# A decoder layer on one core: the next input is split a period earlier, and its first projection is done in two blocks around the turning of the second norm's inputs

## The reference

```
i, f, g = x Wi, x Wf, x Wg
a = sigmoid(f);  b = silu(i) * (1 - a);  h[t] = a[t] h[t-1] + b[t]
xg = h * silu(g);  y = xg * rsqrt(mean(xg^2) + 1e-5) * w_norm
x1 = layernorm(x + y Wo)
x2 = layernorm(x1 + wkv(w, u, key=x1, value=ctx))        # a scan over tokens, numerator / denominator
xq = 8-bit rounding of x2 by row;  weights rounded by row too
hid = silu(xq Wgate) * (xq Wup), rounded by row;  out = layernorm(x2 + hid Wdown)
```

## Time and profile before

| | us |
|---|---|
| three runs | 439.98, 434.78, 437.27 (median 437.27) |
| the profiled execution | 435.36 |
| its span, first to last instruction | 433.4 |
| PE busy in the span | 376.4 (87%) |
| DVE busy | 365.8 (84%) |
| ACT busy | 320.0 (74%) |
| POOL busy | 234.0 (54%) |

### The profile page before, as it was taken

One profiled execution on the slowest core, in us unless ns is written; L12 is line 12 of the kernel. 1 busy time (PEld: TensorE's weight loads), 2 busy tenths in 40 slices (PEclk: granted clock), 3 DMA queues, 4 the chain that ended last, 5 costly groups with the idle time before them and its releaser, 6 DMA issues.

```text
span 433.4 us, 7988 instructions
## 1 busy us (share of the span) xinstructions
PE 376.4 (87%) x2810; PEld 292.3 (67%) x2810; DVE 365.8 (84%) x620; ACT 320.0 (74%) x422; POOL 234.0 (54%) x282
## 2 busy tenths in 40 slices
PE   7799889789898899889997999899989997576872
PEld 7797889687865687659764976497648774232331
DVE  3889797575998799989898988898898989899584
ACT  3687777649827898588858995799668975985571
POOL 1775554542644844766475746594459436635451
PEclk9999999989999999999999999999999999889998
DMA  7946550662020010020203020302030202000101
GB/s 253 363 167 238 164 187 2 232 66 75 2 98 1 2 42 33 24 99 0 74 1 122 3 73 2 121 0 73 0 121 0 73 0 73 24 2 0 49 24 52
DMA packets 12843, 31.75 MB, mean 73 GB/s; under 512 B 2038, under 2 KB 5132, under 8 KB 12812
## 3 DMA queue, kind: packets, MB, share of 16 engines
q1 hardware_dynamic: 12812, 31.35, 21.9%
HBM read 27.14 MB, written 4.21 MB: 72 GB/s over the span
## 4 chain that ended last, share of the span: by engine, by line
ACT 22%; DVE 21%; PE 20%; issue 19%; POOL 12%; DMA 3%; SPq 1%; POOLq 0%; ACTq 0%; DVEq 0%
PE proj_ps L478 15%; POOL ring L1266 3%; PE slot_ps L579 2%; POOL x_low L1189 2%; ACT L978 2%; ACT hqT L943 2%; DVE inp L1459 2%; ACT ring L929 2%; ACT L982 2%; DVE stats L1486 2%; DMA ring<-w_gate_up_dram 2%; ACT turn_ps L883 2%; DMA ring<-w_down_dram 2%; POOL gate L1206 1%; DVE x_max L1575 1%
## 5 line engine op out<-in xcount | busy, mean ns | idle before, releaser
L579 PE MATMUL slot_ps<-w1q,xqT 128*128 128x512 bf16 (+1 forms) x384 | 83.1, 367 | 10.3 <-ACT xqT L920 7.6
L1266 POOL TENSOR_TENSOR ring<-ring 128x512 f32<-128x512 f32 (+1 forms) x48 | 60.5, 1262 | 25.7 <-ACT ring L929 25.7
L579 PEld LDWEIGHTS slot_ps<-w1q,xqT 128*128 128x128 bf16 x384 | 36.7, 99 | 48.7 <-issue 8.1
L478 PE MATMUL proj_ps<-x_high,proj_high 128*128 128x256 f32 x384 | 65.0, 291 | 5.0 <-DVE inp L1478 3.1
L478 PE MATMUL proj_ps<-x_low,proj_high 128*128 128x256 f32 x384 | 62.4, 284 | 0.0
L478 PE MATMUL proj_ps<-x_high,proj_low 128*128 128x256 f32 x384 | 62.0, 283 | 0.0
L478 PEld LDWEIGHTS proj_ps<-x_high,proj_high 128*128 128x128 f32 x384 | 53.4, 190 | 8.1 <-issue 7.1
L478 PEld LDWEIGHTS proj_ps<-x_low,proj_high 128*128 128x128 f32 x384 | 53.3, 191 | 0.0
L478 PEld LDWEIGHTS proj_ps<-x_high,proj_low 128*128 128x128 f32 x384 | 53.2, 190 | 0.0
L929 ACT ACTIVATE ring<-ring,zero_bias,x_scale 128x512 f32<-128x512 f32 (+1 forms) x48 | 36.9, 772 | 13.5 <-DVE ring L1598 13.4
L612 PE MATMUL slot_ps<-w2q,hqT 128*128 128x512 bf16 x176 | 42.5, 390 | 4.5 <-ACT hqT L943 3.5
(11 more groups left out here) (135 smaller groups left out, 849.5 us busy)
## 6 DMA issues: line engine op xcount, KB each, us to landing
ring<-w_gate_up_dram SPq DMA_DIRECT2D x11, 512.0 KB, 5.1
forget<-xT_dram SPq DMA_DIRECT2D x8, 512.0 KB, 3.8
x_sb<-x_dram SPq DMA_DIRECT2D x8, 512.0 KB, 4.0
c_sb<-cT_dram SPq DMA_DIRECT2D x8, 512.0 KB, 4.3
out_dram<-z SPq DMA_DIRECT2D x16, 256.0 KB, 2.1
ring<-w_down_dram SPq DMA_DIRECT2D x4, 704.0 KB, 5.4
scale_rows<-scratch_dram SPq DMA_DIRECT2D x2, 704.0 KB, 7.1
x<-wfT_dram SPq DMA_DIRECT2D x2, 512.0 KB, 5.7
```

What stands on the lines that cost most here:

```text
L478: last = nc.tensor.matmul(out, a, b, start=(i == 0), stop=(i == len(terms) - 1))
L579: last = nc.tensor.matmul(slot_ps[:, s, half * 512:half * 512 + width], xqT[:, par, d, t * P:(t + 1) * P], w1q[:, d, half * I + at:half * ...
L1266: nc.gpsimd.tensor_tensor(hid, hid, gate_buf[:, at:at + width], ALU.mult).then_inc(hid_ready, 1)
```

## The change

The split of the input of batch `b + 3` is moved from the head of period `b + 1` to the end of period `b`. On ACT it stands behind the last silu of the period; on POOL behind the last `hidden` and ahead of `rstd_1`. On PE, project 0 of that batch is taken out from behind the third chunk of `mlp_up` and cut in its two blocks: the first ahead of `turn_inputs`, the second behind it. On SP the load of the turned input goes from the head of a period to its second half, and the load of `c` comes first. The loops over periods 2 to 5 become written-out periods, so that all waits are against constants. The number of matmuls, activations and loads stays the same.

```diff
@@ sync @@
             def iteration(b):
-                load_xT(b + 2)
                 load_c(b + 1)
+                load_x(b + 2)
                 store(b * TB - 2, b - 1, 0)
-                load_x(b + 2)
+                if b + 3 < BATCHES:
+                    load_xT(b + 3)
                 store(b * TB - 1, b - 1, 1)
...
-            with sp.Fori(1, BATCHES - 2) as b:
+            load_xT(3)
+            for b in range(1, BATCHES - 2):
                 iteration(b)
@@ tensor @@
-            def project(b, k):
+            def project(b, k, blocks=(0, 1)):
...
-                if k == 0:
+                if k == 0 and blocks[0] == 0:
                     pe.wait_ge(x_high_ready, b + 1)
                     pe.wait_ge(x_low_ready, b + 1)
...
-                for j in range(2):
+                for j in blocks:
...
-                last.then_inc(proj_done, 1)
+                if blocks[-1] == 1:
+                    last.then_inc(proj_done, 1)
@@ tensor, iteration @@
                 mlp_up(b, par, 0, [2])
-                project(b + 2, 0)
                 project(b + 2, 1)
...
                 mlp_down(n, 0)
+                if b + 3 < BATCHES:
+                    project(b + 3, 0, (0,))
                 turn_inputs(b + 1)
+                if b + 3 < BATCHES:
+                    project(b + 3, 0, (1,))
@@ tensor, prologue @@
             mlp_down(0, 0)
-
-            iteration(1, 1)
-            with pe.Fori(2, BATCHES - 2, 2) as b:
-                iteration(b, 0)
-                iteration(b + 1, 1)
+            project(3, 0)
+
+            for b in range(1, BATCHES - 2):
+                iteration(b, b % 2)
@@ scalar, iteration @@
-                split_x(b + 2)
                 silu(b, par, 0, [0])
...
                 silu(b, par, 1, [2])
+                if b + 3 < BATCHES:
+                    split_x(b + 3)
                 normalise_3(n - 1, 1)
@@ scalar, prologue @@
             square(2)
+            split_x(3)
```

More of the change, by code:

```diff
@@ L492, in project @@
                         pe.wait_ge(ig_low, 2 * m - 1 + half)
[L493 to L496, removed]
-                for j in range(2):
+                if blocks[0] == 0:
+                    if k < 2:
+                        wait(pe, z1_ready, b * TB - TB + k + 1)
+                    else:
+                        pe.wait_ge(proj_read, b * PROJ + k - 1)
+                for j in blocks:
                     e = slice((half * 2 + j) * P, (half * 2 + j + 1) * P)
```

## The result

| | before | after |
|---|---|---|
| runs, us | 434.78 to 439.98 (4), median 436.43 | 446.1 to 447.97 (4), median 446.26 |
| profiled execution | 435.36 | 446.11 |
| its span | 433.4 | 444.1 |
| granted clock, mean | 0.980 | 0.966 |
| PE / DVE / ACT / POOL busy, us | 376.4 / 365.8 / 320.0 / 234.0 | 383.4 / 364.9 / 319.4 / 237.3 |

Ratio 1.0225, 95% interval 1.0181 to 1.0269: **slower**, though the interval leaves open whether by more than 2%. The forecast was 445.0, with 434 to 450.

The account below looks back on a forecast made before the run. PE and DVE were taken as nearly full, with the chain through every period's gating multiply. Longer periods (5.7 us) and the prologue (2.0) gave +7.7 on the median of 437.27: 445.0 us, range 434 to 450.

Parts of the forecast that it names:

- The late x_low and the new order on PE: Turn of each period: PE waits 2.12 us for `x_low`, up product 3.29 late, period 1.4 longer; 5.7 in all.
- The clash in the prologue: POOL's new subtraction and DVE's normalisation of x2 exclude each other; the pair exceeds 3 us, gating 1 comes 2.0 later.
- alone it costs nothing: Prologue and period 1: project 0 of batch 3 (2.95 us on PE) delays the third scaling 1.4, covered by waits.
- The waits on DVE: Between third scaling and gating, DVE's 2.70 us of waits are slack that the late up product can use up.
- The clock: PE's clock behind the new 2.12 us pause: taken to hold, since a pause of 2.18 showed no fall.
- rival 3: PE's clock falls in the new pause, 1.6 us or more for each of four periods: 451 to 457, chance 0.05.
- Written-out periods: Loops over periods 2 to 5: jumps and register waits cost nothing; 0, bounds -0.15 a period and +1 in all.
- Rival 1: PE sets the pace and its 2.19 us of pauses a period get filled: faster, 426 to 429, chance 0.12.
- Rival 2: No change: an up product less than about 1.9 us late is absorbed by DVE's waits; 434 to 441, chance 0.17.

Follow-up runs that it names:

- Experiments 1 and 5: Each against the changed kernel: 1 puts POOL's split ahead of the last `hidden`, 439.12 us; 5 subtracts only half the channels for batches 3 to 7, 436.86 us.
- Experiment 4: Changed kernel with POOL's split ahead of the last `hidden`, run without and with a prologue wait for DVE's normalised x2 before the subtraction: 440.58 and 436.05 us.
- experiment 2: Changed kernel with 34 dummy transposes on PE between the down product and the first block of project 0: 443.33 us.
- experiment 6: Kernel before the change with only its loops over periods 2 to 5 written out on all queues: 435.35 us, ratio 0.997.
- Experiment 9: Kernel of early split with project 0 late, plus subtraction ahead of the last `hidden` and project 0's first block between turning and up product: 429.74 us.
- experiment 3: Changed kernel with one added wait: POOL's prologue subtraction starts only after DVE has written both tiles of normalised x2; 445.41 us.
- experiment 8: Changed kernel with project 0 whole at its old place behind the third up chunk, plus POOL's prologue wait for normalised x2: 431.81 us.

## Why the prediction was right, and what it missed

**The late x_low and the new order on PE: right.** The pause was 2.14 (forecast 2.12), the subtraction 2.35, and from the up product to the third scaling it was 243.80 - 237.96 = 5.84, as forecast. From the third scaling to the gating it was 22.20 (forecast 22.21), which is partly luck: 0.40 of a wait that was to go is left, and the scans of `p_state`, taken at their old length, are 0.40 shorter. The pause came out right the same way: from `x_low` to PE's start it was 0.10 (232.86 to 232.96) instead of the 0.24 of the text, and the down product ended 0.16 earlier against the gating. Where the clock held, the block started 3.48 before the up product (forecast 3.56) and the period grew by 1.35 (forecast 1.5). Experiments 1 and 5 move `x_low` (in experiment 1 the last `hidden` goes behind it) and the period follows it one to one.

**The clash in the prologue: right.** The pair took 3.04, over the 3 us named as the sign, and the stretch grew by 2.52, or by 2.00 where the clock held (forecast 2.04). Experiment 4 shows that it costs time: 4.5 us in the medians. What was missing is that PE's wait behind it (2.84) can bring the clock down too. The Trainium skill, "SBUF — State Buffer", section "SBUF: two separate sides", has the lock that makes one engine wait for the other's whole instruction; the 2.04 us are what was left of a subtraction of 2.38 when the pair was due, up to 0.3. The sentence "alone it costs nothing" on project 0 in the prologue fits: with the wait, the stretch is 48.78 to before's 48.82.

**The waits on DVE: nearly.** Those for the gate and the first scan are gone, but 0.40 of the wait for the third norm is left, which was to go.

**The clock: wrong size.** This is the term that failed. The text compared the pause of 2.12 with one of 2.18 that had done no harm and gave the fall 0.05, priced at 1.6 us or more for each of four turns. It happened in three turns of four and cost 1.48 each, 4.4 us in all by the profile (experiment 2; 2.9 between the medians). So what rival 3 describes came on top of the forecast, at a smaller price than its 451 to 457. With it left out, three periods would have grown by 1.20 (46.15 - 44.95) where 1.4 was forecast. One harmless pause near the end of the program was weak evidence: in this kernel, pauses of 2.1 us and the same order of work had both outcomes. The forecast's terms add up to 7.7; the trace has 2.52 + 1.35 + 8.05 = 11.9 in the same stretches. That the forecast came within 1.3 us of the result is in part luck: the stretch ahead of them was 1.16 shorter in the profile after. And the forecast added 1.9 for the distance of the median from the profiled execution, which after the change is only 0.15 (446.26 and 446.11). Together these two make up 2.9 of the 4.2 us that its terms lack.

**Written-out periods: wrong by little.** 0 was taken, with a bound of -0.15 a period. In experiment 6 the first three distances of its profile are 0.18, 0.34 and 0.33 shorter, though its time is not to be told from before. The failing step was to look for the cost of the loop only where the jump is: the second distance has no jump and gains as much. Against 44.62 the changed kernel's 46.15 is 1.53 longer. If the written-out code gains as much in it as in experiment 6, which no run separates, the late up product cost a little more than the forecast's 1.4 and the code gave the difference back.

**Rival 1 (PE's pauses filled)** decides at an `x_low` that is 2 us earlier. The changed kernel does not have it. Experiment 9 has it ready within 0.1 us of the end of the turning, and is faster, with one further edit: the turning stays first. Its 429.7 lies just over the 426 to 429 that the rival gave. **Rival 2** needed an up product less than 1.9 late; from the gating it was 18.08 (172.22 to 190.30) at full clock and 19.59 (218.37 to 237.96) behind the fall, where it was 15.00, so 3.1 and 4.6 late.

**Open:** why the clock held in one turn and fell in three with the same pause and order, and held in a different one in experiment 3. Nothing in the rows of these turns tells them apart, and no run here varied it alone. The Trainium skill, "TensorE: Matmul & The Clock Gate", section "HAM oscillation — how this bites in real kernels", finds falls behind longer idle gaps than these; here the measurement decides, 2.14 us was enough in three turns of four. Which part of experiment 9's gain over experiment 8 (2.1 us between the medians, with intervals that overlap; 0.8 a period in the profiles) is the block's place and which the earlier `x_low` was not taken apart either, nor what in the hardware loop costs the 0.33, nor why the scans of `p_state` are shorter.

## What to carry to other kernels

Before filling a bubble with work, ask when that work's input is ready: work put ahead of the critical step in an ordered queue makes the step wait for the slowest input of both. Put it behind the step that others wait for, into the shadow of the answer, and move its producer early first. And price a merged pause twice: two short pauses (0.49 and 1.28) became one of 2.14, and the long one also cost the clock in three turns of four.

## What the hardware showed that was not expected

- **Granted clock.** A pause of 2.14 us on PE was followed by about 3 us at half clock in three turns of four, by none in the other; 2.84 us in the prologue by a fall in three profiles of five that have the clash whole (0.57, 0.67 and 0.50 in their windows of 4 us). With pauses of 1.20 and 1.07, and with dummies in the pause, it held in every turn. In the order before, with 0.65 and 1.21 us close together, it fell in one turn of experiment 6's profile, and the up product there took 5.31 instead of 3.63 us.
- **DVE and POOL.** DVE's normalisation of a pair (two instructions, 1.00 us) took 3.04 behind a POOL subtraction of 2.38 that had begun 0.07 earlier. Behind half a subtraction (1.29 us) it took 1.96.
- **Written-out code.** A period took 44.62 instead of 44.95 us with nothing changed but the loops, in one profile each; the medians (435.35 and 436.61) do not tell the two kernels apart.
